# Turning the second half's token blocks with VectorE and memory, and making their parts beside the first four pairs

## The reference

```
xn  = layernorm(x)                                   # 2048 rows of 512
q, k, v = silu(xn Wqkv^T), 16 heads of 128           # 4 sequences of 512 rows seen as 2 x 1024
o   = lightning attention per head: inside a block  (q k^T * decay) v,
      between blocks a 128 x 128 state  kv = decay * kv + k^T v,  o += q kv
o   = norm_w * o * rsqrt(mean(o^2) + 1e-6)
s   = (sigmoid(xn Wg^T) * o) Wout^T                  # 512 columns
f   = xn * sum(top 8 of softmax(xn R^T + b)) + (top 8 weights) @ expert_bias
out = x + s * silu(f)
```

## Time and profile before

| | |
|---|---|
| runs | 1061.83, 1062.56, 1063.66 us; median 1062.56 |
| profiled execution | 1062.85 us, its span from first to last instruction 1061.1 us |
| TensorE busy | 1045.1 us of the span (98%), granted clock 0.999 |
| VectorE, ScalarE, GpSimd busy | 746.6, 512.1, 633.0 us |
| DMA | 128.12 MB, mean 121 GB/s |

### The profile page before, as it was taken

One profiled execution on the slowest core, in us unless ns is written; L12 is line 12 of the kernel. 1 busy time (PEld: TensorE's weight loads), 2 busy tenths in 40 slices (PEclk: granted clock), 3 DMA queues, 4 the chain that ended last, 5 costly groups with the idle time before them and its releaser, 6 DMA issues.

```text
span 1061.1 us, 15974 instructions
## 1 busy us (share of the span) xinstructions
PE 1045.1 (98%) x5612; PEld 893.9 (84%) x5612; DVE 746.6 (70%) x1293; ACT 512.1 (48%) x804; POOL 633.0 (60%) x512
## 2 busy tenths in 40 slices
PE   6999999999999999999999999999999999999998
PEld 5988888888888888888878888888888888888886
DVE  6847757676766768768667777766767666776867
ACT  5846362553536335453554635445453543545344
POOL 3738374665747557474655957657474755847526
PEclk9999999999999999999999999999999999999999
DMA  7273525435252442527766364352525334253442
GB/s 245 80 277 100 144 60 131 104 99 120 60 136 64 129 90 64 143 68 172 241 208 174 99 152 132 105 114 61 143 70 134 91 99 98 67 124 91 127 131 81
DMA packets 260064, 128.12 MB, mean 121 GB/s; under 512 B 223376, under 2 KB 223760, under 8 KB 259984
## 3 DMA queue, kind: packets, MB, share of 16 engines
q1 hardware_dynamic: 259984, 127.09, 44.0%
HBM read 86.95 MB, written 40.11 MB: 120 GB/s over the span
## 4 chain that ended last, share of the span: by engine, by line
PE 90%; issue 3%; DVE 2%; POOL 2%; DMA 1%; SPq 1%; ACT 0%; POOLq 0%; DVEq 0%; ACTq 0%
PE st_ps L558 17%; PE st_ps L560 17%; PE st_ps L559 17%; PE score_ps L680 5%; PE out_ps L733 5%; PE out_ps L735 5%; PE out_ps L734 5%; PE head_ps L716 5%; PE head_ps L719 4%; PE tk_ps L699 4%; PE st_ps L546 1%; PE st_ps L547 1%; PE st_ps L548 1%; DMA xt_lo<-spill_lo 1%; POOL acc L1578 1%
## 5 line engine op out<-in xcount | busy, mean ns | idle before, releaser
L558 PE MATMUL st_ps<-xt_hi,w_hi 128*128 128x512 f32 x826 | 336.6, 407 | 1.0 <-DMA xt_lo<-spill_lo 0.8
L560 PE MATMUL st_ps<-xt_hi,w_lo 128*128 128x512 f32 x826 | 323.2, 391 | 0.0
L559 PE MATMUL st_ps<-xt_lo,w_hi 128*128 128x512 f32 x826 | 322.1, 390 | 0.0
L1467 POOL TENSOR_TENSOR w_lo<-land_a,w_hi 128x1024 fp32r<-128x1024 f32 x44 | 107.3, 2439 | 131.5 <-ACT w_hi L1060 131.5
L560 PEld LDWEIGHTS st_ps<-xt_hi,w_lo 128*128 128x128 f32 x826 | 155.0, 188 | 34.4
L558 PEld LDWEIGHTS st_ps<-xt_hi,w_hi 128*128 128x128 f32 x826 | 155.5, 188 | 30.5 <-issue 1.6
L559 PEld LDWEIGHTS st_ps<-xt_lo,w_hi 128*128 128x128 f32 x826 | 155.7, 189 | 27.9
L1447 POOL TENSOR_TENSOR w_lo<-land_a,w_hi 128x768 fp32r<-128x768 f32 x44 | 83.8, 1905 | 146.4 <-ACT w_hi L1055 146.4
L733 PE MATMUL out_ps<-wo_hi,gate_hi 128*128 128x512 f32 x240 | 96.2, 401 | 0.6 <-DVE acc L1784 0.6
L1786 DVE TENSOR_TENSOR acc<-acc,out_ps 128x512 f32<-128x512 f32 x104 | 71.2, 685 | 32.5 <-PE out_ps L735 32.2
L1498 POOL TENSOR_TENSOR acc_sq<-acc_sq,square 128x512 f32<-128x512 f32 x61 | 78.3, 1284 | 25.9 <-ACT square L1151 25.9
(11 more groups left out here) (331 smaller groups left out, 2060.1 us busy)
## 6 DMA issues: line engine op xcount, KB each, us to landing
land_a<-wgrp_dram SPq DMA_DIRECT2D x48, 512.0 KB, 3.7
v_row<-v_squares SPq DMA_DIRECT2D x120, 128.0 KB, 3.2
k_row<-k_squares SPq DMA_DIRECT2D x120, 96.0 KB, 2.9
v_squares<-v_t SPq DMA_DIRECT2D x45, 256.0 KB, 2.8
land_b<-wo_dram SPq DMA_DIRECT2D x16, 512.0 KB, 4.5
land_b<-wgrp_dram SPq DMA_DIRECT2D x14, 512.0 KB, 4.2
k_squares<-state SPq DMA_DIRECT2D x15, 384.0 KB, 2.3
k_squares<-v_t SPq DMA_DIRECT2D x15, 384.0 KB, 4.8
```

Source lines behind the costliest of these rows:

```text
L558: pe.matmul(ps[:, :], w_h2, x_h2, start=first and k == 0, stop=False, skip_group_check=True)
L559: pe.matmul(ps[:, :], w_h2, x_l2, start=False, stop=False, skip_group_check=True)
L560: end = pe.matmul(ps[:, :], w_l2, x_h2, start=False, stop=last and k == 1, skip_group_check=True)
L1467: pool.tensor_tensor(flat(w_lo[:, n % 2, 3:7, :, :]), flat(landing(ss, g)), flat(w_hi[:, n % 2, 3:7, :, :]).bitcast(F32), ALU.subtract).th ...
```

## The change

The 16 fills of the second half, their takes, their spills and `token_sum1` are taken out of step 0. In their place:

- DVE turns the eight row tiles of the second half in squares of 32 x 32 (`square_rows`) into four slots `x_turned`, which lie over `gate_hi` and `gate_lo`. SP writes each to memory (`x_back_out`): four ahead of the load of group GATE of step 0, four behind it.
- SP reads each tile of the blocks B11, B12, B22, B21 back with the squares in place (`load_raw`, four DMAs each), into four buffers `raw_block` over `res_row`: two behind the first load of group VAL, then in steps 1, 2 and 3.
- In steps 1 to 4 the parts and sums are made from these buffers, one tile after another: per step four of `take_block` (ACT, high part), `split_block` (POOL, low part) and `spill` (SP, two writes), and `sum_block` (POOL) for T1 in steps 1 and 3 and for T3, T2, T4 in steps 2 and 4. `block_hi` and `block_lo` are one place each (over `top_t`): a `take_block` waits until the parts before it are written.
- `direct_block` goes round three banks instead of two, and `gate_high(0, 0, 0)` and `gate_low(0, 0, 0)` move from step 1 to step 0, where `gate_high` waits for the writes of `x_turned`.

```diff
-        stage_hi = over("stage_hi", [P, SEQ], F32R, ring_base)
-        stage_lo = over("stage_lo", [P, SEQ], F32R, ring_base + 2048)
+        raw_block = [over(f"raw_block{i}", [P, SEQ], F32, ring_base + 2048 * i) for i in range(4)]
+        block_hi, block_lo = (top_t[:, NCH * i:NCH * (i + 1), :].rearrange("e c t -> e (c t)") for i in range(2))
+        MADE = (B11, B12, B22, T1, B21, T3, T2, T4)
+        RAW_OF = {B11: 0, T1: 0, B12: 1, T3: 1, B21: 2, T4: 2, B22: 3, T2: 3}
...
         SP
+            def x_back_out(t):
+                sp.wait_ge(x_squared, t + 1)
+                sp.dma_start(x_squares[t // NCH][t % NCH * P:(t % NCH + 1) * P, :], x_turned[:, t % 4, :]).then_inc(x_out[t % 4], 16)
+            def load_raw(blk, k):
+                b, kt = rows_of(2 * blk + k)
+                i = RAW_OF[blk]
...
+                rows = x_squares[b].rearrange("(c i a) (m e) -> m a c i e", i=4, a=32, e=32)
+                for j in range(4):
+                    sp.dma_start(raw_block[i][32 * j:32 * j + 32, :].rearrange("a (c i e) -> a c i e", i=4, e=32),
+                                 rows[4 * kt + j]).then_inc(raw_in[i], 16)
+            def spill(blk, k):
+                sp.wait_ge(block_l, made_at(blk, k) + 1)
+                sp.dma_start(spill_hi[2 * blk + k], block_hi.bitcast(F32)).then_inc(spilled, 16)
+                sp.dma_start(spill_lo[2 * blk + k], block_lo.bitcast(F32)).then_inc(spilled, 16)
...
                 values_out(ss, 0)
+                if ss in (1, 3):
+                    load_raw(B22, ss // 2)
+                    load_raw(B21, ss // 2)
                 load_group(pair, ss, GATE)
                 load_out(pair, ss)
                 values_out(ss, 1)
                 values_out(ss, 2)
+                if ss <= 4:
+                    spill(MADE[(ss - 1) % 2 * 4], (ss - 1) // 2)
                 values_back(ss, 0)
+                if ss <= 4:
+                    spill(MADE[(ss - 1) % 2 * 4 + 1], (ss - 1) // 2)
                 values_out(ss, 3)
                 values_back(ss, 1)
+                if ss <= 4:
+                    spill(MADE[(ss - 1) % 2 * 4 + 2], (ss - 1) // 2)
...
                 keys_back(ss, 1)
+                if ss <= 4:
+                    spill(MADE[(ss - 1) % 2 * 4 + 3], (ss - 1) // 2)
...
             load_group(0, 0, QK1)
+            for t in range(4):
+                x_back_out(t)
             load_group(0, 0, GATE)
-            for f in range(4):
-                spill(f)
+            for t in range(4, TILES):
+                x_back_out(t)
+            load_out(0, 0)
             load_group(1, 1, QK0)
-            for f in range(4, 10):
-                spill(f)
-            load_out(0, 0)
             load_group(1, 1, VAL)
-            for f in range(10, 16):
-                spill(f)
+            load_raw(B11, 0)
+            load_raw(B12, 0)
             load_group(1, 1, QK1)
         PE
             direct_block(6)
-            fill(1, 3)
-            fill(1, 4)
             v_fill(3)
-            fill(1, 5)
             kv_products(0, 0, 0)
-            fill(1, 6)
...
         ACT
+            def take_block(blk, k):
+                at = made_at(blk, k)
+                if blk in (B11, B12, B21, B22):
+                    act.wait_ge(raw_in[RAW_OF[blk]], 64 * (k + 1))
+                else:
+                    act.wait_ge(block_sum, 4 * k + (T1, T3, T2, T4).index(blk) + 1)
+                if at:
+                    act.wait_ge(spilled, 32 * at)
+                act.activation(block_hi, raw_block[RAW_OF[blk]][:, :], ACT.Copy).then_inc(block_h, 1)
...
                 take_k_rows(ss, odd, 0, 0)
                 take_k_rows(ss, odd, 0, 1)
+                if ss <= 4:
+                    take_block(MADE[(ss - 1) % 2 * 4], (ss - 1) // 2)
...
                 gate_high(before, 0, 1)
                 gate_high(before, 1, 1)
+                if ss <= 4:
+                    take_block(MADE[(ss - 1) % 2 * 4 + 1], (ss - 1) // 2)
...
                     raw_hi(ss, GATE)
                 act_c12(ss, VAL)
                 act_c11(ss, QK1)
+                if ss <= 4:
+                    take_block(MADE[(ss - 1) % 2 * 4 + 2], (ss - 1) // 2)
...
                 act_c21(ss, QK1)
+                if ss <= 4:
+                    take_block(MADE[(ss - 1) % 2 * 4 + 3], (ss - 1) // 2)
...
         POOL, step
                 sums_lo(ss, QK1)
+                if ss in (1, 3):
+                    split_block(B11, ss // 2)
+                    split_block(B12, ss // 2)
+                if ss in (2, 4):
+                    split_block(B21, ss // 2 - 1)
+                    sum_block(T3, ss // 2 - 1)
+                    split_block(T3, ss // 2 - 1)
+                    sum_block(T2, ss // 2 - 1)
...
                 raw_lo(ss, GATE)
                 weight_sums(ss, GATE)
+                if ss in (1, 3):
+                    split_block(B22, ss // 2)
+                    sum_block(T1, ss // 2)
+                if ss in (2, 4):
+                    split_block(T2, ss // 2 - 1)
+                    sum_block(T4, ss // 2 - 1)
...
                 sums_lo(ss, GATE)
+                if ss in (1, 3):
+                    split_block(T1, ss // 2)
+                if ss in (2, 4):
+                    split_block(T4, ss // 2 - 1)
         DVE, step 0
+            def square_rows(t):
...
+                    dve.wait_ge(x_out[t % 4], 16)
+                dve.transpose(x_turned[:, t % 4, :], row_tile(1, t // NCH, t % NCH)).then_inc(x_squared, 1)
...
             take_fill(11)
+            square_rows(0)
+            square_rows(1)
             score_decay(0, 0, 0)
-            take_fill(1, 0)
             query_decay(0, 0, 0)
-            take_fill(0, 12)
-            take_fill(0, 13)
-            take_fill(1, 1)
+            square_rows(2)
+            square_rows(3)
+            take_fill(12)
+            take_fill(13)
+            square_rows(4)
+            square_rows(5)
```

More of the change, by code:

```diff
@@ L145, in lightning_block @@
         v_out, v_in = [sem("v_out0"), sem("v_out1")], [sem("v_in0"), sem("v_in1")]
-        spilled = [sem("spilled0"), sem("spilled1"), sem("spilled2")]
+        x_out, raw_in = [sem(f"x_out{i}") for i in range(4)], [sem(f"raw_in{i}") for i in range(4)]
+        spilled = sem("spilled")
         block_in = [sem(f"block_in{i}") for i in range(8)]
@@ L243, in rows_of, with fill_bank @@
             return b, 2 * half + f % 2
[L245 to L255, removed]
+        def fill_bank(f):
+            return (out_ps, tk_ps, score_ps, head_ps)[f % 4] if f < 8 else (out_ps, head_ps)[f % 2]
         def direct_bank(j):
-            return st_ps[j] if j < 3 else st_ps[(j + (j < 12)) % 2]
+            return st_ps[j % 3] if j < 12 else st_ps[j % 2]
         def direct(j):
@@ L269, in row_tile, with made_at @@
             return late_row[:, c, :] if b else gated[:, c // 2, c % 2, :]
-        def stage(f):
-            if f % 3 < 2:
-                return gate_hi[:, f % 3, :], gate_lo[:, f % 3, :]
-            return stage_hi[:, :], stage_lo[:, :]
+        def made_at(blk, k):
+            return 8 * k + MADE.index(blk)
         def value_bank(f):
@@ L878, in _ @@
             for f in range(4):
-                fill(0, f)
+                fill(f)
             direct_block(0)
@@ L1162, in gate_high @@
                     act.wait_ge(out_full, TILES * ss)
+                elif ss == 0 and b == 0 and h == 0:
+                    for slot in x_out:
+                        act.wait_ge(slot, 32)
                 if b == 1:
@@ L1203, in step @@
                 act_c11(ss, QK0)
-                if first:
-                    for i in range(3):
-                        act.wait_ge(spilled[i], 32 * (16 // 3 + (i == 0)))
-                    gate_high(0, 0, 0)
                 gate_high(before, 1, 0)
@@ L1563, in _ @@
             mask_decay(0)
-            for i in range(3):
-                token_sum1(i)
             direct_lo(2, 0)
             direct_lo(2, 1)
-            token_sum1(3)
             raw_lo(1, QK0)
@@ L1839, in take_top @@
                 dve.wait_ge(top_turned, 2 * bp + half + 1)
+                if bp == 0 and half == 0:
+                    dve.wait_ge(spilled, 32 * 16)
                 dve.tensor_copy(top_t[:, NCH * half:NCH * (half + 1), :].rearrange("e c t -> e (c t)"),
```

243 lines of the change are left out of this document (95 added, 148 removed).

## The result

| | before | after |
|---|---|---|
| median of 6 runs, us | 1062.70 (1061.83 to 1063.66) | 1067.89 (1065.70 to 1069.93) |
| ratio after / before, 95% interval | | 1.0048 [1.0032, 1.0063] |
| profiled execution / its span, us | 1062.85 / 1061.1 | 1069.26 / 1067.5 |
| mean granted clock of TensorE | 0.999 | 0.995 |

The change makes the kernel 5.2 us slower, 0.5%. The forecast was 1061.0 us, and the range ended at 1066.5: the time lies outside it, on the side of rival B.

The account below looks back on a forecast made before the run. PE was taken as the bound, busy 98% of the span. Off 7.5 us (6.4 + 0.4 + 0.7), on 5.9 (0.3 + 5.6): 1062.56 - 1.6 = 1061.0 us, range 1056.0 to 1066.5.

Parts of the forecast that it names:

- rival B: Staging buffer in steps 1 to 4 costs more than the transposes did: low write lands at 5.0 us, 1068.0 us; chance 0.17.
- Fills: Step 0: sixteen fills of four transposes leave PE, 0.40 us each, 6.4 us off (5.6 to 7.0).
- DVE in front of PE: Step 1: 0.4 us off at the product block after 83.68, 0.7 us at the output block waiting for acc.
- Gate weights of step 0: Step 0: load issued ten us later, behind four x_back_out writes, landing at 47.8; 0.5 us of cover, 0.3 us charged.
- Rival C: Step 0: gate weights land 7.9 us after issue and stall v_fill(3) 3.7 us, 1064.4 us; chance 0.09.
- The single staging place: Steps 1 to 4: second take_block waits for the first spill, delaying PE's output block 5; 5.6 us on (1.8 to 14.2).
- loss = landing time of the low write - 1.84 us: PE's loss before output block 5: 1.76 us each in steps 1 and 3, 1.06 each in steps 2 and 4.
- Nothing is charged for POOL: Steps 1 to 4: the 24 new POOL instructions could each hold DVE up to 1.28 us by the shared port; 0 charged.
- rival D: Port lock: one POOL instruction met by each gate_low of four steps, 5.1 us, 1066.1 us; chance 0.05.
- SP's eight raw reads: Steps 1 and 3: 5.3 us on SP ahead of the gate load, making two loads start 3 us later.
- The test for "wrong altogether": The prediction would be wrong altogether if PE waited in a step after the fourth.

Follow-up runs that it names:

- run 1: Changed kernel without the copies, splits, sums and spills of steps 1 to 4 and without all raw reads: 1056.37 us, 0.9939 of the kernel before.
- run 2: Changed kernel with the parts going in turn to two staging places with a semaphore each: 1061.18 us, 0.9984 of the kernel before.
- run 3: Changed kernel with the second, third and fourth take_block of each step, and their splits and spills, moved later: 1058.66 us, 0.9957 of the kernel before.
- run 5: Changed kernel with SP's order and bytes kept, ACT and POOL without the new work, spills writing first-half tiles: 1061.80 us, 0.9983 of the kernel before.
- run 6: run 5 without the 32 raw reads, its spill writes kept: 1055.46 us, 0.9929 of the kernel before.
- run 4: Changed kernel with the eight raw reads of steps 1 and 3 behind the first spill, not ahead of the gate load: 1066.64 us, 1.0036.
- run 7: run 5 without the 32 spill writes, its raw reads kept: 1057.70 us, 0.9951 of the kernel before.
- run 11: Changed kernel with copies and spills moved later, step 0's gate weights loaded first, B21 read at the end of steps 1 and 3: 1055.32 us, 0.9931.

## Why the prediction was wrong, point by point

- **Fills, 6.4 us off: right.** 6.1 us by the first block of step 1, with 0.40 of the new stall in it: 6.5.
- **DVE in front of PE, 0.4 + 0.7 us off: half right.** The wait on acc of the earlier trace rows went, 0.74 us. The 0.4 did not come: the product block behind the matmul of 77.32 now waits 0.44 us for state, 0.24 us more than before. I had followed only q_t there, and not what DVE does for the product beside it.
- **Gate weights of step 0, 0.3 us: right in place, small by luck.** They were issued at 44.66 and landed at 48.75 (forecast 44.1 and 47.8); PE lost 0.40 us here, but 1.2 to 1.5 us in runs 1, 2, 3, 5 and 6, whose step 0 up to there is the same, and 0.5 and 0.1 us in runs 4 and 7. Rival C's 3.7 us did not come.
- **The single staging place, 5.6 us on: the mechanism right, the size too small.** "loss = landing time of the low write - 1.84 us" gives, with the times from issue to ACT's release, 3.73, 3.16, 5.48 and 2.64 us, losses of 1.89, 1.32, 3.64 and 0.80; PE waited 1.86, 1.20, 3.57 and 0.68. The term that was wrong is the landing, taken as 3.6, 2.9, 3.6 and 2.9: 0.1, 0.3 and 1.9 us too small and once 0.3 too long, and with the restart behind each wait 7.95 us where 5.6 stood. In step 3 the low write was issued 4 us behind the loads and 0.6 us behind v_squares, in the stretch that showed 337 GB/s before and has 368 and 395 in the windows above; I had put the median there, where the same argument pointed to the long end of the earlier trace rows. The mean, 3.75 us, is just beyond the 3.6 from which rival B decides. By B's sum it would still be only 1063; B's 1068.0 stands for a mean landing of 5.0 us.
- **The clock: missing.** 4.4 us. The step that failed is "PE loses" the length of the wait and nothing more: the sum has no term for what the matmuls behind it lose. The forecast for the profiled execution was 1061.25 us and it took 1069.26, 8.0 more: 4.4 for the clock, 2.6 for the four waits and their restarts, 1.0 for the rest. The median of the runs, where the miss is 6.9 us, holds executions with a mean clock of 0.995 to 0.998, so the clock's part differs from one to the next. The clock of 0.999 over the whole span gave no hint, but the trace of before did, in the starts behind its gap of 9.7 us:

```profile
10.70 1.06 PE L509 MATMUL tk_ps<-consts,acc 128*128 128x128 f32 x4
11.56 1.06 PE L509 MATMUL score_ps<-consts,acc 128*128 128x128 f32 x4
...
13.70 0.63 PE L547 MATMUL st_ps<-xt_lo,w_hi 128*128 128x512 f32 x1
14.12 0.45 PE L548 MATMUL st_ps<-xt_hi,w_lo 128*128 128x512 f32 x1
```

  A fill there takes 0.86 us to the next and not the 0.44 of the earlier trace rows, and a block matmul 0.42 and not 0.23, although the granted clock reads 1.00 in these windows. Matmuls behind a long gap were seen to be slow; from which length on was not.
- **"Nothing is charged for POOL": right.** By the Trainium skill (SBUF — State Buffer, "SBUF: two separate sides") a GpSimd instruction and a VectorE one with two SBUF inputs lock each other out; the mean gate_lo did rise from 1072 to 1305 ns in the changed kernel. But run 11 has the same POOL work, a mean of 1160 ns, and of PE's waits none that run 1, without that work, doesn't have: rival D fell.
- **SP's eight raw reads: too long by themselves, but underpriced.** They held SP for 4.2 us and not 5.3, and the loads in step 3 came 1.7 us later and not 3. But I let them act through the spill's landing only. Runs 5 to 7 show that with the spills they cost 5.4 us on another path, v_squares and v_row. In the changed kernel PE shows no wait there, since the waits on acc make it late itself: taking these away (run 2) uncovered the second path.
- **The test for "wrong altogether": met by its letter, badly put.** PE waits 0.69 us at 643, in the second half, where the kernel before does not wait. But run 1, which has none of the parts' work, waits 0.50 us at the same product, so this is not of the spills; the four waits of steps 1 to 4 came where they were looked for.

## What to carry to other kernels

A transfer between two users of one buffer is not priced by the median landing: look at what the same queue issues in the few microseconds ahead of it, and take the long end when weight loads stand there. On a TensorE that is never idle the price of a new wait is not its length alone: here none of 31 waits up to 1.6 us was followed by half clock, and all four of 1.9 to 2.2 us were, at 1.5 us or more each. Before adding a buffer, move the waiting copy behind the work that others need: by the medians the order of the copies and spills was worth 9.2 us here, with that of the reads and one load 12.6, and the second buffer 6.7.

## What the hardware showed that I had not expected

- A TensorE wait of 1.9 to 3.8 us can be followed by 4 to 12 matmuls at 1.2 GHz (pitch 0.43 instead of 0.23 us), starting within 1.3 us of the wait's end; it costs 1.5 to 2.8 us beyond the wait. Waits of the same length at the same place in a step differ in it, and run 5's executions lie between 1057.37 us with a mean clock of 1.00 and 1064.73 with 0.997.
- The same write of 256 KB takes 2.6 to 5.4 us from issue to landing in the changed kernel. The Trainium skill (DMA: Bandwidth & Descriptors, "Anatomy of one DMA — SWDGE (gpsimd) path", the two cost components) gives, for a DMA issued from GpSimd, a fixed part of about 2.0 us and bytes over the bandwidth, by its figures an estimate of 2.6 us. These writes are issued by SyncE; their least agrees with it, and the most is twice that, behind 1 MB of loads and 64 KB reads in small packets.
- Two kinds of traffic that alone made PE wait 0.86 us in step 1 and 1.13 us in step 3 made it wait 0.95 and 2.12 us together, with 1.6 us of half clock behind the last: 5.4 us by the medians, where each alone was within the noise.
